# Down products of the last expert: rows 0 and 1 beside the up products, rows 2 and 3 behind them, one by one

## The chip, the cores and the metric

One core of one Trainium2 chip runs the whole program in one launch. The metric is the device time of one execution in microseconds (us); less is better. The core has five engines that run their own instruction streams and meet through semaphores: TensorE (PE in the profile, with its weight loads as PEld), VectorE (DVE), ScalarE (ACT), GpSimd (POOL) and SyncE (SP), the last of which starts most DMAs. An indirect DMA (one whose rows are addressed by a list of indices) is started by GpSimd.

## The reference

The input x is 4 sequences of 1024 tokens with 256 columns. Four steps follow, each on the layer norm of x and added to x: a mixing step, an expert step, causal attention, and the same expert step again.

```
def ffn(x, gate_w, w1, w2):            # n=4 sequences, t=1024, d=256, e=8 experts, k=256
    probs = softmax(einsum('ntd,ed->nte', x, gate_w))
    g, m = top_k(probs.transpose(0, 2, 1), k)      # each expert takes its best 256 tokens
    xin = x[batch_idx, m]                          # of each sequence
    h = gelu(einsum('nekd,edf->nekf', xin, w1))    # "up": 256 -> 1024
    h = einsum('nekf,efd->nekd', h, w2)            # "down": 1024 -> 256
    return zeros.at[batch_idx, m].add(g[..., None] * h)
x = x + mix(norm(x));  x = x + ffn(norm(x), ...)   # layer 0
x = x + attn(norm(x)); x = x + ffn(norm(x), ...)   # layer 1
```

The change lies in the last part of the second expert step.

## The kernel before

**Tiling of the expert step.** The four sequences are taken in two pairs. One pass n (0 to 15 in a layer) is one expert (n % 8) for one pair of sequences (n // 8): 512 gathered tokens, in four row groups j = 0 to 3 of 128 tokens each. Row groups 0 and 1 belong to the first sequence of the pair, 2 and 3 to the second. "The last expert" is the pass n = 15 of layer 1, the last work of the kernel.

**One pass.** The 1024 hidden columns are done in FT = 8 blocks f of 128.

- `up` (line 1311 holds its matmuls): for one f, 6 matmuls with 512 moving columns (2 halves of the 256 input columns, 3 products each, since each number is kept as a high and a low part) into PSUM bank 2 or 3 in turn, for all four row groups at once. ScalarE then takes the gelu out of the bank (line 1685), and VectorE writes the high part (2167) and the low part (2169) of h.
- `down` (line 1332): for one f, 4 row groups times 3 products = 12 matmuls with 256 moving columns. They add up over f = 0 to 7 in PSUM: row groups 0 and 1 in the two halves of bank 4, row groups 2 and 3 in those of bank 5. The first `down` of a pass waits (`take`) until both banks are drained; each `down` waits for the low part of h of its f.
- TensorE's order is written out in `experts`: `down` of f - 3 comes behind `up` of f (LAG = 3), so up 0, 1, 2, 3, down 0, up 4, down 1, up 5, down 2, up 6, down 3, up 7, down 4, 5, 6, 7. With the last `down`, bank 4 is signalled as filled behind the sixth of its 12 matmuls and bank 5 behind the twelfth.
- `scatter`: for each row group j, ScalarE multiplies the 128x256 result by the gate values into a tile f_yo (line 1694), and GpSimd starts an indirect DMA that adds its rows onto the output in HBM (line 2388). Row groups 0 and 1 wait for bank 4, row groups 2 and 3 for bank 5. GpSimd waits for ScalarE: for an even j through a count of its own (a_yo), for an odd j through the "drained" count of the bank. Before the first it also waits until the adds of the pass before have landed.

In every pass but the last the scatter stands beside the next pass's products. In the last one nothing comes behind it but the barrier: SyncE waits until all adds have landed (`stores_done`), each engine drains (line 428), and the program ends.

**Names.** `k.where[key]` says which bank a key such as ("down", layer, n, half) was given and as which use of it; `wait_filled` and `wait_drained` wait on that use. Bank 6 serves the routing of the pairs (route_ring) until that is over, and is not used in the last passes.

Of the kernel before, what the change touches and what calls it, by code (L numbers as in the profile page):

```python
# [15 lines left out]
P = 128  # L16
# [32 lines left out]
class Kernel:  # L49
# [282 lines left out]
    def tiles(self):  # L332
# [13 lines left out]
        self.t["early"].update({n: second[n] for n in ("tab", "idx", "row")})  # L346
        self.f = (first, second)

    def turned_block(self, t, i):

        flat = t["yT"][:].rearrange("p k l -> p (k l)")[:, i % 4 * BANK:(i % 4 + 1) * BANK]
        return flat.rearrange("p (s k l) -> p s k l", s=2, k=self.DT)
# [35 lines left out]
class Program:  # L388
# [26 lines left out]
    row_turn = row_scores = half_wide = count = digits = thresholds = threshold_rows = compare = rank = positions = skip  # L415
    hot_digits = hot_places = column = table = skip
    table_move = indices = skip
    weight_load = weight_high = weight_split = gather = xin = up = down = scatter = skip
    first_rows = rows_store = t_load = skip
    xt_block = qk_load = v_load = qk_product = qk_low = qk_double = v_product = skip  # L420
    row_max = part_max = max_rows = high_scores = scores = weigh = add_up = divide = sum_rows = scale_rows = skip
# [226 lines left out]
    def experts(self, layer, routed, gathered, turned):  # L648

        k, t = self.k, self.k.f[layer]  # L650
        LAG, N, FT = 3, 2 * k.E, k.FT
        if not gathered:
            self.gather(layer, 0, t)
        for _ in self.weights_ahead:
            pass
        if not turned:
            self.xin(layer, 0, t)
        yield
        for n in range(N):
            if n + 1 < N:  # L660
                routed(2 * layer + (n + 1) // k.E)
                self.gather(layer, n + 1, t)
            if n:
                for j in range(4):
                    self.scatter(layer, n - 1, j, t)
            for f in range(FT + LAG):
                if f < FT:
                    self.up(layer, n, f, t)
                    yield
                if f == FT - 1 and n + 1 < N:  # L670
                    self.xin(layer, n + 1, t)
                    self.turned = n + 1
                if f >= LAG:
                    self.down(layer, n, f - LAG, t)
                    yield
                part = f - LAG
                if 0 <= part < 4 and n + 1 < N:
                    self.weight_high(layer, n + 1, part, t)
                    self.weight_split(layer, n + 1, part, t)
                    if part % 2 and n + 2 < N:  # L680
                        self.weight_load(layer, n + 2, part // 2, t)
            self.through += 1
        for j in range(4):
            self.scatter(layer, N - 1, j, t)

    def stage_f(self, layer, before, behind):

        k, t = self.k, self.k.f[layer]
        self.norm_of, self.routed, self.loaded, self.through = {}, -1, 0, 0
        self.turned = 0  # L690
        first, second = iter(()) if layer else self.route(0), self.route(2 * layer + 1)
        self.weights_ahead = self.first_weights(layer)
        self.route_ring = [6, 7]
        gathered = turned = False
        self.route_uses = 1
        for n, _ in enumerate(before):
            pump(first)
            if layer and (n == 16 or 22 < n < 31 and n % 2 or n > 41):
                pump(self.weights_ahead)
            if self.routed == 2 * layer and not gathered and (layer == 0 or n > 41):  # L700
                self.gather(layer, 0, t)
                gathered = True
            if layer and n == 48:
                self.xin(layer, 0, t)
                turned = True
        for n, _ in enumerate(first):
            if n % 3 == 0 and self.loaded == 0:
                pump(self.weights_ahead)
        self.route_uses = 0

        def later():
            yield from second
            if layer == 0:
                while self.through < k.E:
                    yield
                self.first_rows()
                for _ in range(4):
                    yield
                self.norm_of["t", 0] = self.runs
                for _ in self.norm(k.t["xy"], k.t["xy"], t["stats"][0], t["mv"][0], t["rstd"][0], [(k.q_x, DMA)]):  # L720
                    for _ in range(4):
                        yield
            yield from behind
        later = later()

        def routed(r):
            while self.routed < r:
                next(later)
        for n, _ in enumerate(self.experts(layer, routed, gathered, turned)):
            pump(later)  # L730
        for _ in later:
            pass
# [296 lines left out]
class TensorE(Program):  # L1029
# [285 lines left out]
    def down(self, layer, n, f, t):  # L1315
# [20 lines left out]
        if f < FT - 1:  # L1336
            m.then_inc(k.pe_down, 1)

    def xt_block(self, b, c, dt):
# [192 lines left out]
class ScalarE(Reader):  # L1534
# [152 lines left out]
    def scatter(self, layer, n, j, t):  # L1687
        k, act = self.k, self.e
        b, h = 2 * (n // k.E) + j // 2, j % 2
        bank = self.wait_filled(("down", layer, n, j // 2))  # L1690
        if n:
            last = 2 * ((n - 1) // k.E) + j // 2
            self.wait_ge(k.q_add[last][h], DMA * (k.E * layer + (n - 1) % k.E + 1))
        act.mul(t["yo"][j][:], k.bank[bank][:, h * k.D:(h + 1) * k.D],
                t["tab"][b][:, n % k.E, h, 1:2]).then_inc(k.drained[bank] if h else k.a_yo, 1)
# [562 lines left out]
class GpSimd(Reader):  # L2258
# [114 lines left out]
    def scatter(self, layer, n, j, t):  # L2373
        k, pool = self.k, self.e
        b, h, e = 2 * (n // k.E) + j // 2, j % 2, n % k.E
        if h:
            self.wait_drained(("down", layer, n, j // 2))
        else:
            self.wait_ge(k.a_yo, 2 * (2 * k.E * layer + n) + j // 2 + 1)
        if e:  # L2380
            for i in range(2):
                self.wait_ge(k.q_add[b][i], DMA * (k.E * layer + e))
        elif layer:
            for c in range(k.NC):
                self.wait_ge(k.q_xout[c], DMA * (b + 1))
        else:
            self.wait_rows_stored(b // 2)
        pool.indirect_dma_start(
            out=(k.out if layer else k.res)[:, :],
            out_offset=bass.IndirectOffsetOnAxis(ap=t["row"][b][:, e, h:h + 1], axis=0),  # L2390
            in_=t["yo"][j][:], in_offset=None, compute_op=ALU.add).then_inc(k.q_add[b][h], DMA)
# [290 lines left out]
```

## Time and profile before

| what | us |
|---|---|
| median of the runs | 2219.75 (2218.33 to 2220.87, 3 runs) |
| the profiled execution: its own time | 2221.76 |
| its span in the trace | 2220.0 |
| PE busy in the span | 2142.3 (97%) |
| POOL busy in the span | 1374.8 (62%) |
| mean granted TensorE clock | 0.989 of full speed |

The profiled execution took 2221.76 us by the same clock as the runs; the trace covers 2220.0 of it, so 1.76 us lie around the span. Times below count from the span's start. Of a matmul the trace gives the start and a modelled end; successive matmuls overlap in it, so the distance between two starts is what one costs in a row of them.

### The profile page before, as it was taken

The page shows a single profiled execution, that of the slowest core. Times are in us where ns is not written, and L with a number is a line of the kernel's source. Part 1 is how long each engine was busy: PE and PEld are TensorE (multiplying, and loading weights), DVE is VectorE, ACT ScalarE, POOL GpSimd, SP SyncE. Part 2 cuts the span into 40 slices and gives each one's busy share as a digit, 9 for nine tenths or more (in the row PEclk, how much of TensorE's full clock was granted, in tenths as well). Part 3 has the DMA queues.
Part 4 walks back from the last instruction along what each step waited for, and adds up shares of the span by engine and source line. Part 5 has one row for each costly group of instructions (what it writes and reads, how often), then busy time and mean ns, then how long its engine had stood idle before and what let it go on. Part 6 is the DMA issues. An engine that isn't in the chain of part 4 may idle for free.

```text
span 2220.0 us, 34078 instructions
## 1 busy us (share of the span) xinstructions
PE 2142.3 (97%) x12130; PEld 1597.7 (72%) x12130; DVE 1463.3 (66%) x3344; ACT 1002.8 (45%) x1908; POOL 1374.8 (62%) x1242
## 2 busy tenths in 40 slices
PE   7998999999999999999999999999999999999997
PEld 5446888889876666766667666567666588899997
DVE  7375687776757666476775577874876646975553
ACT  6302543454355555255553355542555425444442
POOL 4313675777357676466664566663777846777774
PEclk9999999999999999999999999999999899999999
DMA  4524554555432221221222132222221245545552
GB/s 133 185 95 127 140 134 103 142 141 134 98 92 58 58 58 49 67 77 51 75 70 74 39 86 50 56 67 64 61 77 30 67 135 130 139 111 132 136 143 29
DMA packets 145048, 206.04 MB, mean 93 GB/s; under 512 B 19432, under 2 KB 112112, under 8 KB 144880
## 3 DMA queue, kind: packets, MB, share of 16 engines
q1 hardware_dynamic: 120304, 170.30, 25.7%
q0 software_dynamic: 24576, 33.57, 9.1%
q8 instruction: 97, 1.59, 0.3%
q14 instruction: 71, 0.58, 0.1%
HBM read 130.03 MB, written 39.85 MB: 77 GB/s over the span
## 4 chain that ended last, share of the span: by engine, by line
PE 74%; DVE 8%; POOL 4%; issue 3%; ACT 2%; DMA 1%; SPq 1%; POOLq 0%; DVEq 0%; ACTq 0%
PE psum L1311 12%; PE psum L1332 11%; PE psum L1458 11%; PE psum L1360 8%; PE psum L1423 7%; PE psum L1439 6%; PE psum L1483 5%; PE psum L1374 4%; PE psum L1388 3%; PE psum L1468 3%; POOL t_acc L2430 2%; DVE f_hlo L2169 1%; DVE f_hhi L2167 1%; PE psum L1401 1%; PE psum L1279 1%
## 5 line engine op out<-in xcount | busy, mean ns | idle before, releaser
L1734 ACT ACTIVATE t_p<-psum 128x512 f32<-128x512 f32 (+3 forms) x768 | 323.6, 492 | 294.1 <-PE psum L1439 285.8
L2430 POOL TENSOR_TENSOR t_acc<-t_acc,t_p 128x1024 f32<-128x1024 f32 (+3 forms) x256 | 417.0, 1629 | 14.5 <-ACT t_p L1734 0.5
L2349 POOL TENSOR_TENSOR f_wlo<-f_wst,f_whi 128x256 fp32r<-128x256 f32 x256 | 222.1, 944 | 149.8 <-ACT f_whi L1667 149.8
L1332 PE MATMUL psum<-f_whi,f_hhi 128*128 128x256 f32 x1024 | 295.4, 288 | 7.9 <-DVE f_hlo L2169 7.8
L1458 PE MATMUL psum<-t_p,t_v 128*64 128x512 f32 (+3 forms) x1536 | 289.1, 497 | 5.0 <-POOL t_p L2410 5.0
L1332 PE MATMUL psum<-f_whi,f_hlo 128*128 128x256 f32 x1024 | 289.9, 283 | 0.0
L1332 PE MATMUL psum<-f_wlo,f_hhi 128*128 128x256 f32 x1024 | 289.7, 283 | 0.0
L2167 DVE CAST f_hhi<-f_h 128x512 fp32r<-128x512 f32 x256 | 141.2, 552 | 207.0 <-ACT f_h L1685 206.2
L1685 ACT ACTIVATE f_h<-psum 128x512 f32<-128x512 f32 x256 | 153.0, 598 | 275.6 <-PE psum L1311 263.1
L1423 PE MATMUL psum<-t_qa,t_ka 128*128 128x512 f32 (+3 forms) x768 | 224.3, 372 | 1.8 <-DVE t_mx L2215 0.8
L2430 POOL TENSOR_TENSOR t_acc<-t_p 128x768 f32<-128x768 f32 x64 | 134.5, 2102 | 137.0 <-PE psum L1468 133.7
L1458 PEld LDWEIGHTS psum<-t_p,t_v 128*64 128x64 f32 x1536 | 99.2, 137 | 159.4 <-issue 141.3
L2410 POOL TENSOR_SCALAR_AFFINE_SELECT t_p<-t_p 128x256 f32<-128x256 f32 x256 | 105.0, 420 | 174.8 <-ACT t_p L1734 174.1
L1439 PE MATMUL psum<-t_qb,t_kb 65*128 65x512 f32 (+3 forms) x768 | 207.3, 352 | 4.8 <-DMA t_qb<-t_neg 4.4
L1311 PE MATMUL psum<-f_xhi,f_whi 128*128 128x512 f32 x512 | 204.8, 400 | 7.0 <-DVE f_xlo L2153 3.8
L1332 PEld LDWEIGHTS psum<-f_whi,f_hhi 128*128 128x128 f32 x1024 | 195.3, 191 | 16.7 <-DVE f_hlo L2169 9.6
L2169 DVE TENSOR_TENSOR f_hlo<-f_h,f_hhi 128x512 fp32r<-128x512 f32 x256 | 199.7, 780 | 8.8
L1311 PE MATMUL psum<-f_xlo,f_whi 128*128 128x512 f32 x512 | 202.1, 395 | 0.0
L1311 PE MATMUL psum<-f_xhi,f_wlo 128*128 128x512 f32 x512 | 201.0, 393 | 0.0
L1332 PEld LDWEIGHTS psum<-f_wlo,f_hhi 128*128 128x128 f32 x1024 | 195.4, 191 | 4.8
L1332 PEld LDWEIGHTS psum<-f_whi,f_hlo 128*128 128x128 f32 x1024 | 195.3, 191 | 0.0
L2221 DVE TENSOR_REDUCE t_mx<-psum 128x1 f32<-128x512 f32 x256 | 159.6, 683 | 41.5 <-PE psum L1388 38.9
(291 smaller groups left out, 4401.6 us busy)
## 6 DMA issues: line engine op xcount, KB each, us to landing
f_wst<-in_L_ffn_w SPq DMA_DIRECT2D x64, 1024.0 KB, 5.5
t_ka<-t_ka SPq DMA_DIRECT2D x64, 256.0 KB, 3.5
t_qb<-t_qa SPq DMA_DIRECT2D x64, 256.0 KB, 3.8
t_wk<-wkT SPq DMA_DIRECT2D x32, 256.0 KB, 4.1
t_wq<-wqT SPq DMA_DIRECT2D x32, 256.0 KB, 4.0
t_wv<-wvT SPq DMA_DIRECT2D x16, 512.0 KB, 4.7
normal<-f_xy SPq DMA_DIRECT2D x5, 1024.0 KB, 5.6
a_x<-in_L_attn_a_x SPq DMA_DIRECT2D x4, 1024.0 KB, 7.8
```

The source lines that it names most:

```text
L1311: m = pe.matmul(k.bank[b], w[:, dt, fs], x[:, dt, :], start=(dt == 0 and j == 0), stop=(dt == k.DT - 1 and j == 2))
L1332: m = pe.matmul(out, h[:, js], w[:, f, :], start=(f == 0 and a == 0 and j % 2 == 0), stop=(f == FT - 1 and a == 2), skip_group_check=True)
L1360: m = pe.matmul(k.bank[bank], w[:, part, ct, :], x[:, ct, cs], start=(ct == 0 and a == 0), stop=(ct == 1 and a == 2))
L1423: pe.matmul(k.bank[bank][:, q0:], hd["ka"][:, ks], hd["qa"][:, qs], start=True, stop=False)
L1439: pe.matmul(k.bank[banks[i]][:, q0:], hd["kb"][0:k.QROWS, ks], hd["qb"][0:k.QROWS, qs], start=False, stop=True).then_inc(k.filled[banks[i] ...
L1458: m = pe.matmul(k.bank[6][i * DH:(i + 1) * DH, q0:BANK], v[:, kt, vs:vs + DH], p[:, i, q0:BANK], start=(kt == 0), stop=(kt == last), skip_ ...
L1734: act.activation(p[:, i, q0:], k.bank[bank][:, q0:], ACT.Exp, scale=1.0 / float(np.sqrt(k.DH))).then_inc(k.drained[bank], 1)
L2167: dve.tensor_copy(hhi[:], h[:]).then_inc(k.d_h.sem, 1)
L2169: dve.tensor_tensor(hlo[:], h[:], hhi[:].bitcast(F32), ALU.subtract).then_inc(k.d_h.sem, 1)
L2221: s = dve.tensor_reduce(mx1[:, i, n - k.KPC:n - k.KPC + 1], part, AX.X, ALU.max)
L2349: m = pool.tensor_tensor(t["wlo"][n % 2][:, i, ks], t["wst"][:, i, ks], t["whi"][n % 2][:, i, ks].bitcast(F32), ALU.subtract)
L2430: pool.tensor_tensor(acc[:, :, q0:], (p0 if kt == 1 else acc)[:, :, q0:], p[:, :, q0:], ALU.add).then_inc(k.p_acc, 1)
```

## The change

The passes before the last one stay as they are. In the last one (layer 1, n = 15), `experts` calls `last_expert`:

- beside the up products, with the same lag of 3, only row groups 0 and 1 of the down products are done (6 matmuls per f in place of 12);
- behind up 7 come: row groups 0 and 1 for f = 4 (within the loop), 5 and 6; row group 2 for f = 0 to 3; row groups 0 and 1 for f = 7; row group 2 for f = 4 to 7; row group 3 for f = 0 to 7;
- row group 2 stays in bank 5, row group 3 goes into bank 6, each signalled as filled when its own f = 7 is done. ScalarE and GpSimd wait for row group 3 by the key of bank 6;
- the number of matmuls and their shapes stay the same. The count pe_down is not raised in this pass; only a next pass would wait for it.

```diff
+    def down_key(self, layer, n, j):
+        return "down", layer, n, 2 if layer and n == 2 * self.E - 1 and j == 3 else j // 2
...
                 for j in range(4):
                     self.scatter(layer, n - 1, j, t)
+            if layer and n == N - 1:
+                yield from self.last_expert(layer, n, t)
+                continue
...
+    def last_expert(self, layer, n, t):
+        LAG, FT = 3, self.k.FT
+        for f in range(FT):
+            self.up(layer, n, f, t)
+            yield
+            if f >= LAG:
+                self.down_rows(layer, n, f - LAG, (0, 1), t)
+                yield
+        for f in range(FT - LAG, FT - 1):
+            self.down_rows(layer, n, f, (0, 1), t)
+        for f in range(4):
+            self.down_rows(layer, n, f, (2,), t)
+        self.down_rows(layer, n, FT - 1, (0, 1), t)
+        for f in range(4, FT):
+            self.down_rows(layer, n, f, (2,), t)
+        for f in range(FT):
+            self.down_rows(layer, n, f, (3,), t)
...
+    def down_rows(self, layer, n, f, js, t):          # TensorE
...
+        key = k.down_key(layer, n, js[0])
+        if f == 0:
+            self.take(key, 4 + key[3])
...
+        self.wait_ge(k.d_h.sem, k.d_h.at(FT * N + f, "lo"))
+        for j in js:
+            out, rows = k.bank[bank][:, (j % 2) * D:(j % 2 + 1) * D], slice(j * P, (j + 1) * P)
+            for a, (h, w) in enumerate(((t["hhi"][f], w2h), (t["hhi"][f], w2l), (t["hlo"][f], w2h))):
+                m = pe.matmul(out, h[:, rows], w[:, f, :], start=(f == 0 and a == 0 and j == js[0]),
+                              stop=(f == FT - 1 and a == 2), skip_group_check=True)
+        if f == FT - 1:
+            m.then_inc(k.filled[bank], 1)
...
     def scatter(self, layer, n, j, t):                # ScalarE
-        bank = self.wait_filled(("down", layer, n, j // 2))
+        bank = self.wait_filled(k.down_key(layer, n, j))
...
     def scatter(self, layer, n, j, t):                # GpSimd
         if h:
-            self.wait_drained(("down", layer, n, j // 2))
+            self.wait_drained(k.down_key(layer, n, j))
```

## Rows read from the trace of the kernel before

**Rows 1.** The page: busy time of the engines, and busy tenths in 40 slices

```profile
PE 2142.3 (97%) x12130; PEld 1597.7 (72%) x12130; DVE 1463.3 (66%) x3344; ACT 1002.8 (45%) x1908; POOL 1374.8 (62%) x1242
...
PE   7998999999999999999999999999999999999997
```

**Rows 2.** The chain of work that ended last, from 2180 us: start, us, what

```profile
2200.17 1.39 PE psum L1311 x6
2201.55 5.05 PE psum L1332 x42
2206.60 0.02 issue
2206.62 0.48 ACT f_yo L1694
...
2212.93 1.55 POOL out L2388
```

**Rows 3.** Timeline of GpSimd, the last two passes' scatters: start, us, what, idle before

```profile
2190.47 1.76 POOL L2388 DMA_INDIRECT out<-f_yo,f_row  x1 [0.30 <-DMA out<-f_yo,f_row]
2207.37 1.55 POOL L2388 DMA_INDIRECT out<-f_yo,f_row  x1 [15.14 <-ACT f_yo L1694]
2209.22 1.55 POOL L2388 DMA_INDIRECT out<-f_yo,f_row  x1 [0.30 <-issue]
2211.08 1.55 POOL L2388 DMA_INDIRECT out<-f_yo,f_row  x1 [0.30 <-issue]
2212.93 1.55 POOL L2388 DMA_INDIRECT out<-f_yo,f_row  x1 [0.30 <-issue]
```

**Rows 4.** Drains at the end (line 428), then the first instruction behind the barrier: count, ns

```profile
L428 PEldq DRAIN  x1: 2345/2345/2345, 2205.0 to 2205.0; - x1
...
L428 POOLq DRAIN  x1: 10987/10987/10987, 2208.5 to 2208.5; - x1
L428 SPq DRAIN  x1: 7/7/7, 2216.7 to 2216.7; - x1
...
L2654 SPq COMPARE_BRANCH  x1: 38/38/38, 2219.5 to 2219.5; - x1
```

**Rows 5.** Timeline of TensorE, the last pass: up 7, then down 7's first, sixth, last

```profile
2200.00 0.40 PE L1311 MATMUL psum<-f_xhi,f_whi 128*128 128x512 f32 x1
...
2201.16 0.39 PE L1311 MATMUL psum<-f_xhi,f_wlo 128*128 128x512 f32 x1
2201.39 0.28 PE L1332 MATMUL psum<-f_whi,f_hhi 128*128 128x256 f32 x1
...
2205.70 0.28 PE L1332 MATMUL psum<-f_whi,f_hhi 128*128 128x256 f32 x1
2205.82 0.28 PE L1332 MATMUL psum<-f_wlo,f_hhi 128*128 128x256 f32 x1
2205.94 0.28 PE L1332 MATMUL psum<-f_whi,f_hlo 128*128 128x256 f32 x1
2206.06 0.28 PE L1332 MATMUL psum<-f_whi,f_hhi 128*128 128x256 f32 x1
...
2206.30 0.28 PE L1332 MATMUL psum<-f_whi,f_hlo 128*128 128x256 f32 x1
...
2207.02 0.28 PE L1332 MATMUL psum<-f_whi,f_hlo 128*128 128x256 f32 x1
```

**Rows 6.** Busy time by stretch (PE, PEld, DVE, ACT, POOL), granted clock, DMA share, GB/s

```profile
2201.40:2207.30 5.90, 5.90 (x49) 5.70 (x47) 1.12 (x2) 1.27 (x3) 0.00 (x0) 1.00 0.00 0
...
2216.00:2217.00 1.00, 0.00 (x0) 0.00 (x0) 0.00 (x0) 0.00 (x0) 0.00 (x0) 0.50 0.10 13
2217.00:2218.00 1.00, 0.00 (x0) 0.00 (x0) 0.00 (x0) 0.00 (x0) 0.00 (x0) 0.50 0.00 0
```

**Rows 7.** Timelines of ScalarE and VectorE, the last pass: gelu and h of f = 7, the scatter

```profile
2201.59 0.60 ACT L1685 ACTIVATE f_h<-psum 128x512 f32<-128x512 f32 x1 [2.22 <-PE psum L1311]
2206.62 1.57 ACT L1694 ACTIVATE f_yo<-psum,f_tab 128x256 f32<-128x256 f32 x4 [4.44 <-PE psum L1332]
...
2202.29 0.43 DVE L2167 CAST f_hhi<-f_h 128x512 fp32r<-128x512 f32 x1 [1.67 <-ACT f_h L1685]
2202.75 0.69 DVE L2169 TENSOR_TENSOR f_hlo<-f_h,f_hhi 128x512 fp32r<-128x512 f32 x1
```

**Rows 8.** DMAs issued from 2203 to 2212 us, then from 2212.9: count, us to landing

```profile
out<-f_yo,f_row POOLq DMA_INDIRECT x3, 3.7
...
out<-f_yo,f_row POOLq DMA_INDIRECT x1, 3.7
```

**Rows 9.** Instructions on f_yo from 2100 us: ns min/median/max, then landing

```profile
L2388 POOL DMA_INDIRECT out<-f_yo,f_row x21: 1548/1760/1795, 2098.3 to 2212.9; - x21
L1694 ACT ACTIVATE f_yo<-psum,f_tab x20: 466/474/479, 2114.0 to 2207.7; 128x256 f32<-128x256 f32 x20
...
DMA to landing us min/median/max: 3.7/4.0/5.2
```

More of the change, by code:

```diff
@@ L417 @@
     table_move = indices = skip
-    weight_load = weight_high = weight_split = gather = xin = up = down = scatter = skip
+    weight_load = weight_high = weight_split = gather = xin = up = down = down_rows = scatter = skip
     first_rows = rows_store = t_load = skip
@@ L1337, in down @@
             m.then_inc(k.pe_down, 1)
+    def down_rows(self, layer, n, f, js, t):
+        k, pe = self.k, self.e
+        D, FT = k.D, k.FT
+        N = 2 * k.E * layer + n
+        key = k.down_key(layer, n, js[0])
+        if f == 0:
+            self.take(key, 4 + key[3])
+            self.wait_ge(k.d_split, 2 * N + 2)
+            self.wait_ge(k.p_split, 2 * N + 2)
+        bank, _ = k.where[key]
+        w2h = t["whi"][n % 2][:, 1].rearrange("p (k d) -> p k d", k=FT)
+        w2l = t["wlo"][n % 2][:, 1].rearrange("p (k d) -> p k d", k=FT)
+        self.wait_ge(k.d_h.sem, k.d_h.at(FT * N + f, "lo"))
[6 more added lines that the diff above has]
+            m.then_inc(k.filled[bank], 1)
     def xt_block(self, b, c, dt):
```

## The prediction

> **What bounds the kernel now.** The page comes first: TensorE is busy for 97% of the span [rows 1], so nearly everywhere the time is its stream of matmuls, and of that stream the change removes nothing. The last of the 40 slices of PE is not full, though: at 55.5 us a slice, the tenth that is missing has to be looked for at the end. So the chain of waits comes second, read from its end backwards [rows 2]: TensorE until 2206.60, one product of ScalarE (the gate of row group 0), then GpSimd to 2212.93 + 1.55 = 2214.48. The third view is GpSimd's timeline [rows 3]. The reader is to see that its four indirect DMAs stand back to back: 1.55 us each and 0.30 of issue between them, starts 2207.37, 2209.22, 2211.08, 2212.93, a pitch of 5.56 / 3 = 1.853 us. Only the first waits for ScalarE; the other three wait for GpSimd itself. Last come the drains [rows 4]: SP leaves its wait for the adds at 2216.7, GpSimd's drain ends at 2208.5 + 11.0 = 2219.5, and all engines go on at 2219.5.
>
> So the last 13.4 us (2220.0 less 2206.6) are a serial tail: first gate product, four DMA issues in a row, a last piece of 2220.0 - 2214.48 = 5.52 us for landing, drain and end. Its start is set by the moment at which bank 4 (row groups 0 and 1) is full. TensorE itself is full until its last matmul ends at 2207.02 + 0.28 = 2207.30 [rows 5], with no idle time and at a granted clock of 1.00, the 2.4 GHz level [rows 6].
>
> **The change part by part.**
>
> *TensorE's stream.* Before and after there are 48 up and 96 down matmuls in the pass. From 2205.70 to 2207.02 there are 11 distances, 0.120 us for one down matmul; the up ones go (2201.16 - 2200.00) / 5 = 0.232 apart [rows 5]. The sum is the same, so TensorE ends at 2207.30 again if nothing makes it wait. Two things could: banks and h.
>
> *h of f = 7.* Its low part is ready at 2202.75 + 0.69 = 2203.44 [rows 7], which is 2.05 after the end of up 7's issue (2201.39 [rows 5]). After the change up 7 comes earlier by the 4 x 6 = 24 down matmuls that are left out ahead of it (f = 0 to 3), 24 x 0.120 = 2.88: issued by 2198.51, h ready at 2200.56. Between it and the down product that needs it stand 6 x 3 (f = 4, 5, 6 of row groups 0 and 1) + 12 (row group 2, f = 0 to 3) = 30 matmuls, 3.60 us: 2202.11. That leaves 1.55 us, so no wait. For the earlier f the distance is larger (three ups and three short downs, 3 x (1.39 + 0.72) = 6.3 us, against the same 2.05). If that cover were gone, each microsecond of lateness would cost one.
>
> *The up products come closer together*, 1.39 + 0.72 = 2.11 us apart instead of 2.82. Their banks alternate, so one is needed again one up and two short downs after it was filled, 2.8 us, and the gelu that frees it starts 0.20 after the up's issue ended and takes 0.60 [rows 5, 7]. VectorE has 0.43 + 0.69 = 1.12 us of work per f [rows 7]. Both fit.
>
> *Banks.* Bank 5 is now asked for later than before, and ScalarE and GpSimd had emptied it before the issue at 2190.47 [rows 3]; bank 6 was last used by the routing, which was over passes ago. No wait on either, I take 0. A gain is excluded, since TensorE had no idle time to lose; a loss could only be a late bank 6, and it would be the same at the end up to the 1.24 us found below.
>
> *When bank 4 is full.* Behind its last matmul there are now 12 (row group 2, f = 4 to 7) + 24 (row group 3) = 36 matmuls instead of 6. It is full 30 x 0.120 = 3.60 us earlier. By the same distances its last matmul starts at 2207.02 - 36 x 0.120 = 2202.70, ScalarE starts at about 2203.02 (before, 2206.30 to 2206.62 [rows 5, 7]) and GpSimd's first DMA 0.75 later [rows 3, 7], at 2203.77. VectorE did its last work at 2200.56, so it stands beside nothing there. The adds of the pass before, for which GpSimd waits, had their last issue at 2190.47 [rows 3]; with the longest landing of 5.2 [rows 9] that is 2195.7, long done.
>
> *The other three.* Row group 1: ready with the first. Row group 2: its bank is full 24 matmuls before the end, at 2207.30 - 2.88 = 2204.42; with 0.04 to ScalarE and 0.75 more, GpSimd could start at 2205.2, and its turn is at 2203.77 + 2 x 1.853 = 2207.48. Row group 3: full at 2207.30, could start at 2208.09; its turn is at 2203.77 + 3 x 1.853 = 2209.33. So GpSimd's own pace still decides, by 1.24 us, and the last DMA starts at 2209.33 instead of 2212.93: 3.60 us earlier. Moving the first one by more would have bought at most the 4.84 us between 2212.93 and 2208.09; past that TensorE's end decides.
>
> *The price of a DMA issue.* The rows give 1548 to 1795 ns [rows 9]. The short ones are those at the end, with VectorE idle; the one at 2190.47 in between took 1.76 [rows 3]. After the change the first two run beside TensorE's matmuls. I take 1.55, as at 2207.37, because VectorE is idle there too; if TensorE's stream made them long (1.79), four times 0.24 = 0.96 would be lost and 2.6 gained. The lower bound is the pitch as it is; nothing in the rows is shorter than 1548.
>
> *Landing and drain.* The last DMA took 3.7 us to land [rows 8], in a stretch where the queue had only its neighbours, at the same pitch as after. The longest on this path was 5.2 [rows 9], when weights and gathers ran too; none do here. SP's release at 2216.7 is 2.2 after the last issue ended, GpSimd's drain ends 5.0 after it [rows 4]. I take both as tied to the last DMA, so they move by the whole 3.60.
>
> Sum: -3.60 us. The profiled execution's span becomes 2216.4 and its own time 2218.2; the median of the runs shown lies 2.0 below the profiled time and becomes 2219.75 - 3.60 = 2216.15, take 2216.2 (-0.16%).
>
> **The rivals.**
>
> *A: the end is not tied to the last DMA.* GpSimd's drain starts at 2208.5, before three of the four DMAs have been issued, and is shown as 11.0 us long [rows 4]. It starts 0.3 after ScalarE's last gate product (2206.62 + 1.57 = 2208.19 [rows 7]). If that length were the drain's own, the end would hang on the last gate product, which TensorE's unchanged end sets. That product would now be alone: 2207.34 to 2207.81, drain from 2208.1 to 2219.1, gain 0.4 us, time 2219.4. For it: the data have landed at 2216.7 and traffic ends in the slice before 2217 [rows 6], yet the drain goes on for 2.8 us. Against it: it has to outlast work that stands ahead of it in GpSimd's queue. The Trainium skill ("PSUM — Partial Sum Buffer", Engine vs sequencer instructions) says that a drain waits until its engine is fully idle; by that rule the drain is a wait behind the last DMA and the forecast holds, by a fixed length from its own start it would be 2219.4. The trace cannot tell them apart, since there is one such drain.
>
> *B: single row groups run slower (the other side).* Row groups 2 and 3 now put 24 matmuls in a row into one 128x256 region, where before it was 3. If each had to wait for the one before to end, they would go 0.28 apart instead of 0.12 [rows 5], 48 x 0.16 = 7.7 us more: TensorE ends at 2215.0, the last DMA starts at 2215.8, 2.8 later than before, time 2222.6. It decides from a distance at which the 48 cost over 4.84 us, that is 0.22 us apart. Against it: within a group of three the starts are 0.12 apart, just as between groups [rows 5], and up puts six in a row into one region at 0.232, well under their 0.39. Nothing speaks for it.
>
> *C: the first DMAs run long beside TensorE* and the landing takes the median 4.0 in place of 3.7: gain 3.6 - 0.96 - 0.3 = 2.3 us, time 2217.4.
>
> *D: the order is right but some wait on h or a bank delays bank 4* by more than the 1.55 us of slack, say 2 us late: 0.5 us lost, 3.1 gained, time 2216.6. It is inside the forecast's own range.
>
> **How the numbers follow.** The forecast with D has 0.75, C 0.11, A 0.10, B 0.04. The forecast's own range is 2214.9 to 2217.4, the gain of 3.6 with the 1.3 us by which the runs shown lie about their median. A measurement of this kernel tells a change from none at about 0.2%, here 4.4 us. The forecast is 3.6, so it lies within that bound but near it; with the spread of the runs a little over a third of the forecast's share would read as more than 4.4: faster 0.28, slower 0.03 (most of B is itself only 2.8 us), same 0.69. Range with the rivals: 2214.3 to 2218.9, which leaves out A's end and B.
>
> **What would show it.** In the profile after: TensorE without idle time until about 2207.3; ScalarE's first gate product near 2203.0 and its last alone near 2207.3; four DMAs at a pitch of 1.85 from 2203.8, the last at 2209.3 with 0.3 of issue ahead of it and not a wait for ScalarE; SP's release near 2213.1 and GpSimd's drain ending near 2215.9 while it still starts near 2208. A drain that ends near 2219 would be A; down matmuls more than 0.12 apart would be B; issues of 1.75 us C. A wait on VectorE ahead of down 7 would break the step on h.

## The result and the profile after

The changed kernel takes 2216.53 us (median of 18 runs, 2214.75 to 2221.86) against 2220.53 (18 runs, 2218.07 to 2224.3): ratio 0.9984, 95% interval 0.9977 to 0.9990. The ratio stands for 3.6 us; the two medians lie 4.0 us apart. The forecast was 2216.2. Its profiled execution took 2218.82 us, with a span of 2217.0.

GpSimd's timeline after, first the last add of the pass before, then the four of the last pass (start, us, what, idle before). It answers to [rows 3]:

```profile
2191.07 1.76 POOL L2436 DMA_INDIRECT out<-f_yo,f_row  x1 [0.30 <-issue]
2204.37 1.55 POOL L2436 DMA_INDIRECT out<-f_yo,f_row  x1 [11.54 <-ACT f_yo L1742]
2206.22 1.55 POOL L2436 DMA_INDIRECT out<-f_yo,f_row  x1 [0.30 <-issue]
2208.08 1.55 POOL L2436 DMA_INDIRECT out<-f_yo,f_row  x1 [0.30 <-issue]
2209.93 1.55 POOL L2436 DMA_INDIRECT out<-f_yo,f_row  x1 [0.30 <-issue]
```

The same four, at the same pitch, 3.00 us earlier. ScalarE's side of it, answering to [rows 7]:

```profile
2199.31 0.60 ACT L1733 ACTIVATE f_h<-psum 128x512 f32<-128x512 f32 x1 [1.50 <-PE psum L1337]
2203.62 0.84 ACT L1742 ACTIVATE f_yo<-psum,f_tab 128x256 f32<-128x256 f32 x2 [3.72 <-PE psum L1382]
2205.07 0.47 ACT L1742 ACTIVATE f_yo<-psum,f_tab 128x256 f32<-128x256 f32 x1 [0.60 <-PE psum L1382]
2207.94 0.47 ACT L1742 ACTIVATE f_yo<-psum,f_tab 128x256 f32<-128x256 f32 x1 [2.40 <-PE psum L1382]
```

The four gate products have come apart: two when bank 4 is full, one for bank 5, one for bank 6 behind TensorE's end. TensorE's first and last down matmuls in the tail of the pass, and the busy time by stretch (PE, PEld, DVE, ACT, POOL, clock, DMA share, GB/s), answering to [rows 5, 6]:

```profile
2199.11 0.28 PE L1382 MATMUL psum<-f_whi,f_hhi 128*128 128x256 f32 x1
...
2207.62 0.28 PE L1382 MATMUL psum<-f_whi,f_hlo 128*128 128x256 f32 x1
```

```profile
2200.00:2207.90 7.90, 7.90 (x66) 7.70 (x65) 1.12 (x2) 1.31 (x3) 3.10 (x2) 1.00 0.14 17
2207.90:2217.00 9.10, 0.00 (x1) 0.00 (x0) 0.00 (x0) 0.47 (x1) 3.10 (x2) 0.66 0.40 43
```

From 2199.11 to 2207.62 there are 71 distances of 0.120 us; TensorE has no idle time, at a granted clock of 1.00. VectorE made the low part of h for f = 7 here, and the four adds took this long to land:

```profile
2200.47 0.69 DVE L2217 TENSOR_TENSOR f_hlo<-f_h,f_hhi 128x512 fp32r<-128x512 f32 x1
```

```profile
DMA to landing us min/median/max: 3.7/3.8/3.9
```

The drains, answering to [rows 4]:

```profile
L432 POOLq DRAIN  x1: 8031/8031/8031, 2208.5 to 2208.5; - x1
L432 SPq DRAIN  x1: 7/7/7, 2213.8 to 2213.8; - x1
...
L2702 SPq COMPARE_BRANCH  x1: 38/38/38, 2216.5 to 2216.5; - x1
```

GpSimd's drain starts at 2208.5 in both traces, but is 3 us shorter. It starts 0.3 us behind the end of ScalarE's last product again; that product now stands alone, so this is 0.6 us behind TensorE's end where it was 1.2.

TensorE's end T (end of the last matmul) is the fixed point from which such a tail has to be read. It lies at 2207.30 before and at 2207.62 + 0.28 = 2207.90 after, since this execution had come to the last pass 0.60 us later: the eight transposes of the pass start at 2178.18 before (first line) and at 2178.78 here (second):

```profile
2178.18 0.87 PE psum L1292 x8
```

```profile
2178.78 0.87 PE psum L1318 x8
```

The pass itself takes 29.12 us in both. The tail, span less T, is 2220.0 - 2207.30 = 12.70 before and 2217.0 - 2207.90 = 9.10 after: 3.60 us shorter, of which 3.00 show in the span. In the traces of the experiments T lies between 2202.9 and 2213.9, which is more than any edit is worth, while the tail of a kernel traced twice came out alike within 0.1 us (9.10 and 9.11, 7.56 and 7.58). So the tails carry the verdicts, one trace each, and the ratios of the runs only have to agree.

### The profile page after: what moved, and what is told of

It reads as the page before. It is cut to its first block, busy times and chain, and to the rows that moved or that the text cites. A ratio compares the mean times of both kernels' runs of the same rounds, so it can differ in the third digit from the quotient of the medians.

```text
span 2217.0 us, 34079 instructions
## 1 busy us (share of the span) xinstructions
PE 2144.5 (97%) x12130; PEld 1600.3 (72%) x12130; DVE 1463.6 (66%) x3344; ACT 1003.0 (45%) x1908; POOL 1375.0 (62%) x1242
## 4 chain that ended last, share of the span: by engine, by line
PE 74%; DVE 8%; POOL 4%; issue 3%; ACT 2%; DMA 1%; SPq 1%; POOLq 0%; DVEq 0%; ACTq 0%
PE psum L1337 12%; PE psum L1506 11%; PE psum L1358 11%; PE psum L1408 8%; PE psum L1471 7%; PE psum L1487 6%; PE psum L1531 5%; PE psum L1422 4%; PE psum L1436 3%; PE psum L1516 3%; POOL t_acc L2478 2%; DVE f_hhi L2215 2%; DVE f_hlo L2217 1%; PE psum L1449 1%; DVE f_wlo L2190 1%
## 5 line engine op out<-in xcount | busy, mean ns | idle before, releaser
L1358 PE MATMUL psum<-f_whi,f_hhi 128*128 128x256 f32 x992 | 286.4, 289 | 7.1 <-DVE f_hlo L2217 7.0
L1358 PE MATMUL psum<-f_whi,f_hlo 128*128 128x256 f32 x992 | 280.8, 283 | 0.0
L1358 PE MATMUL psum<-f_wlo,f_hhi 128*128 128x256 f32 x992 | 280.6, 283 | 0.0
L1358 PEld LDWEIGHTS psum<-f_whi,f_hhi 128*128 128x128 f32 x992 | 189.1, 191 | 15.6 <-DVE f_hlo L2217 9.0
L1358 PEld LDWEIGHTS psum<-f_wlo,f_hhi 128*128 128x128 f32 x992 | 189.3, 191 | 4.6
L1358 PEld LDWEIGHTS psum<-f_whi,f_hlo 128*128 128x128 f32 x992 | 189.2, 191 | 0.0
```

The costliest lines, as they stand in the source:

```text
L1358: m = pe.matmul(out, h[:, js], w[:, f, :], start=(f == 0 and a == 0 and j % 2 == 0), stop=(f == FT - 1 and a == 2), skip_group_check=True)
```

## The experiments

All but the last start from the changed kernel. What came out, in us; "last add" is the start of the last indirect DMA against T:

| kernel | T | last add | tail | ratio to the kernel before, 95% interval |
|---|---|---|---|---|
| before | 2207.30 | T + 5.63 | 12.70 | 1 |
| changed | 2207.90 | T + 2.03 | 9.10 | 0.9984 (0.9977 to 0.9990) |
| e1 shared bank | 2204.08 | T + 2.64 | 9.72 | 0.9986 (0.9977 to 0.9995) |
| e2 later | 2202.85 | T + 4.19 | 11.25 | 0.9988 (0.9979 to 0.9997) |
| e3 first | 2209.73 | T + 0.79 | 7.87 | 0.9983 (0.9974 to 0.9992) |
| e4 no add of group 1 | 2208.81 | T + 0.78 | 7.79 | 0.9983 (0.9974 to 0.9992) |
| e5 = e3 + e4 | 2211.10 | T + 0.79 | 7.80 | 0.9977 (0.9968 to 0.9986) |
| e6 no adds of groups 2, 3 | 2213.42 | T - 1.68 | 5.98 | 0.9970 (0.9957 to 0.9982) |
| e7 = e3, no last barrier | 2210.14 | T + 0.78 | 7.56 | 0.9979 (0.9969 to 0.9988) |
| e8 changed, again | 2213.89 | T + 2.03 | 9.11 | 0.9982 (0.9973 to 0.9991) |
| e9 no adds in the pass | 2207.18 | none | 5.82 | one run each |
| e10 = e7 + early drain | 2213.89 | T + 0.79 | 5.01 | 0.9968 (0.9956 to 0.9980) |
| e11 = e7, again | 2213.82 | T + 0.78 | 7.58 | 0.9979 (0.9970 to 0.9988) |
| e12 before + early drain | 2205.52 | T + 5.62 | 10.28 | 0.9983 (0.9974 to 0.9992) |

Every interval leaves 1 out, so each version that has one is faster than the kernel before. Every interval also overlaps the changed kernel's, so the runs alone do not tell the versions apart. The times expected of e1 to e4 were 2217.1, 2218.7, 2215.3 and 2215.3; the medians were 2216.74, 2218.16, 2216.50 and 2215.86, so e3 missed its time by 1.2 us though its tail came as expected. In the code cuts below `...` marks what is left out.

**e1_shared_bank: row group 3 back in bank 5.**

```diff
-        return "down", layer, n, 2 if layer and n == 2 * self.E - 1 and j == 3 else j // 2
+        return "down", layer, n, j // 2
...
-        if f == 0:
+        if f == 0 and js[0] != 3:
             self.take(key, 4 + key[3])
...
-        if f == FT - 1:
+        if f == FT - 1 and js[0] != 2:
             m.then_inc(k.filled[bank], 1)
```

The start flag of row group 3 is dropped too. Bank 5 is so taken once, by row group 2, and signalled as filled once, behind the last matmul of row group 3.

> The order of the changed kernel, but row group 3 shares bank 5 with row group 2, signalled once behind the last matmul. Measured from the end of TensorE's last matmul (T), the changed kernel starts its last add at T + 2.03 us and the span ends at T + 9.10. Theory (the end is the later of GpSimd's turn and readiness): ScalarE's products 2 and 3 start at T + 0.04 and T + 0.40, the third add at T + 0.79, the last at T + 2.64; tail 9.7, time 0.6 above the changed kernel's (about 2217.1). Rival (the own bank buys nothing, since GpSimd's pace sets the end): tail 9.1, time unchanged.

GpSimd's third add now waits for ScalarE, and the chain is broken in its middle:

```profile
2202.40 1.55 POOL L2436 DMA_INDIRECT out<-f_yo,f_row  x1 [0.30 <-issue]
2204.86 1.55 POOL L2436 DMA_INDIRECT out<-f_yo,f_row  x1 [0.92 <-ACT f_yo L1742]
2206.72 1.55 POOL L2436 DMA_INDIRECT out<-f_yo,f_row  x1 [0.30 <-issue]
```

The wait is 0.92, of it 0.30 would have been issue anyway: the own bank is worth 0.62 us of the 3.60 (9.72 against 9.10), and the order without it brings the other 2.98.

**e2_later: row groups 0 and 1 finished 18 matmuls later.**

```diff
-        for f in range(4):
+        for f in range(FT):
             self.down_rows(layer, n, f, (2,), t)
+        for f in range(2):
+            self.down_rows(layer, n, f, (3,), t)
         self.down_rows(layer, n, FT - 1, (0, 1), t)
-        for f in range(4, FT):
-            self.down_rows(layer, n, f, (2,), t)
-        for f in range(FT):
+        for f in range(2, FT):
             self.down_rows(layer, n, f, (3,), t)
```

> Row groups 0 and 1 of f = 7 come behind all of row group 2 and two f of row group 3, so that 18 matmuls follow them in place of 36. Theory (GpSimd's chain starts when bank 4 is full, 0.12 us per matmul moved): first add 18 x 0.12 = 2.16 us later against T, last add at T + 4.19, tail 11.3, time about 2218.7 (1.4 us gained on the kernel before). Rival (the gain comes from the banks of their own and the single row groups, not from where row groups 0 and 1 end): tail 9.1, time 2216.5.

```profile
2202.57 0.28 PE L1382 MATMUL psum<-f_whi,f_hlo 128*128 128x256 f32 x1
```

```profile
2207.04 1.55 POOL L2436 DMA_INDIRECT out<-f_yo,f_row  x1 [0.30 <-issue]
```

Tail 11.25 against 9.10: 2.15 us for 18 matmuls, 0.119 each. Banks and single row groups are as in the changed kernel; what is lost hangs on the moment at which bank 4 is full.

**e3_first: row groups 0 and 1 finished at once.**

```diff
-        for f in range(FT - LAG, FT - 1):
+        for f in range(FT - LAG, FT):
             self.down_rows(layer, n, f, (0, 1), t)
-        for f in range(4):
-            self.down_rows(layer, n, f, (2,), t)
-        self.down_rows(layer, n, FT - 1, (0, 1), t)
-        for f in range(4, FT):
+        for f in range(FT):
             self.down_rows(layer, n, f, (2,), t)
         for f in range(FT):
```

> Behind up 7 row groups 0 and 1 are finished at once (f = 4 to 7), then row group 2, then 3: 48 matmuls follow bank 4. Theory: GpSimd's turn for the last add would be T + 0.59, row group 3 is ready at T + 0.79, so the end is now set by TensorE's end: tail 9.10 - 1.24 = 7.9, time about 2215.3. The low part of h for f = 7 is ready 2.05 us behind up 7 and is wanted after 18 matmuls, 2.16 us: no stall. Rival (h is late, TensorE stalls ahead of down 7): TensorE has idle time there and ends later by it, and the gain of 1.2 shrinks by as much; above 1.2 us of stall it is slower than the changed kernel.

```profile
2208.47 1.55 POOL L2433 DMA_INDIRECT out<-f_yo,f_row  x1 [0.30 <-issue]
2210.52 1.55 POOL L2433 DMA_INDIRECT out<-f_yo,f_row  x1 [0.50 <-ACT f_yo L1739]
```

The last add now waits for ScalarE, 0.20 us beyond the usual 0.30: GpSimd's pace has given the end back to TensorE, as worked out. The tail is 1.23 us shorter. The cover over h has shrunk to nothing, which shows in TensorE's timeline as one distance of 0.18 in place of 0.12:

```profile
2202.92 0.28 PE L1379 MATMUL psum<-f_whi,f_hlo 128*128 128x256 f32 x1
2203.04 0.34 PE L1379 MATMUL psum<-f_whi,f_hhi 128*128 128x256 f32 x1
2203.22 0.28 PE L1379 MATMUL psum<-f_wlo,f_hhi 128*128 128x256 f32 x1
```

The pass takes 29.18 instead of 29.12 (2180.55 to 2209.73). The low part of h was ready at 2202.25 + 0.69 = 2202.94:

```profile
2202.25 0.69 DVE L2214 TENSOR_TENSOR f_hlo<-f_h,f_hhi 128x512 fp32r<-128x512 f32 x1
```

Only 0.11 of slack had been counted. So the four f of row group 2 that the changed kernel puts ahead of down 7 save it 0.06 us of TensorE, and cost it 1.23 us of tail.

**e4_no_add_1 and e5_first_no_add_1: one add fewer**, in the order of the changed kernel and in that of e3. The diff is that of e6 below, with (1,).

> The changed kernel without the last pass's add of row group 1 (its gate product and its wait stay; the output lacks that add). Theory (GpSimd's pace of 1.853 us per add sets the last start, up to the 1.24 us at which row group 3's readiness takes over): last add at T + 0.79, tail 7.9, time about 2215.3. Rival (an add costs its full pitch at the end): last add at T + 0.18, which is impossible before its product is there; (the adds are hidden): tail 9.1.

> Row groups 0 and 1 finished at once (as in e3_first) and the last pass's add of row group 1 left out. Theory (both changes shorten the same thing, GpSimd's turn, and past 1.24 us TensorE's end decides): nothing on top of either alone, last add at T + 0.79, tail 7.8 to 7.9. Rival (the two gains are independent): tail 9.10 - 1.24 - 1.3 = 6.6.

The last add in e4:

```profile
2209.59 1.55 POOL L2438 DMA_INDIRECT out<-f_yo,f_row  x1 [0.85 <-ACT f_yo L1742]
```

Tails 7.79 and 7.80. Taking away 1.85 us of GpSimd's work is worth 1.31 on the changed order and nothing on e3's; both run into the same floor, T + 0.79.

**e6_no_add_23: what the drain waits for.**

```diff
+        if layer and n == 2 * k.E - 1 and j in (2, 3):
+            return
         pool.indirect_dma_start(
...
-                    self.wait_ge(k.q_add[b][h], DMA * k.E * 2)
+                    gone = 2 * (b - 2) + h in (2, 3)
+                    self.wait_ge(k.q_add[b][h], DMA * (k.E * 2 - gone))
```

The return stands behind GpSimd's waits and ahead of the add; the other lines make SyncE wait for as many adds as there are. The output lacks the adds left out, here and in e4, e5 and e9.

> The changed kernel without the last pass's adds of row groups 2 and 3; their gate products stay, and GpSimd still waits for them, so that its drain starts where it did, 0.6 us behind TensorE's end (T). Theory (the drain is a wait for the last add: 5.0 us behind the end of its issue, here at T - 0.13): drain ends at T + 4.9, tail 5.4. Rival (the drain takes a length of its own from its start): it ends at T + 8.6 as in the changed kernel, tail 9.1.

Neither number came. The tail was 5.98:

```profile
L432 POOLq DRAIN  x1: 4834/4834/4834, 2214.0 to 2214.0; - x1
L432 SPq DRAIN  x1: 7/7/7, 2215.7 to 2215.7; - x1
```

The rival of a length from its own start (9.1) is out. But the drain ends 5.5 us behind the last issue (2213.29), not 5.0, and 4.8 behind its own start.

**e9_no_add: no add in the last pass at all.** The same edit with (0, 1, 2, 3).

> The changed kernel without any add in the last pass; the gate products and GpSimd's waits for them stay. The last software DMA has then landed some 10 us before GpSimd's drain starts, 0.6 us behind TensorE's end. In the run without the last two adds the drain ended 5.5 us behind the last issue and 4.8 behind its own start, against 5.0 behind the last issue in all others. Theory 1 (once GpSimd's queue is empty the drain takes 4.8 to 5.0 us of its own, landing or not): drain 4.8 us long, tail 5.9. Theory 2 (the drain waits some 3 us behind the last landing): it is under 1 us long, tail about 2.

```profile
2190.34 1.76 POOL L2438 DMA_INDIRECT out<-f_yo,f_row  x1 [0.30 <-issue]
...
L432 SPq DRAIN  x1: 7/7/7, 2194.4 to 2194.4; - x1
...
L432 POOLq DRAIN  x1: 4671/4671/4671, 2207.8 to 2207.8; - x1
```

SyncE sees all adds landed at 2194.4, 13 us before GpSimd's drain starts, and the drain still takes 4.67 us. So in this trace the drain is no wait for landing: it takes 4.7 us of its own, from when GpSimd has nothing else left. The same 4.7 us behind the 0.30 that follow an issue would give the 5.0 behind the last issue in the traces with all four adds.

**e7_first_no_barrier** (and e11, the same kernel again): is it the explicit drain?

```diff
-        self.barrier()
+        self.stores_done(2)
```

> e3_first without the last barrier of the kernel's own: SyncE still waits for all adds, but no engine drains of its own ahead of the program's end. Theory (the 2.8 us between the last landing and the end of GpSimd's drain belong to GpSimd's queued adds, whichever drain asks for them; the program's end drains too): tail 7.9 less at most the 0.5 us of the second round, 7.4 to 7.9. Rival (the explicit drain itself costs them): tail 7.9 - 2.8 = 5.1.

> e7_first_no_barrier once more on the same chip as e10: tail 7.56, time 1.5 us below the changed kernel's, so about 0.9978 of the kernel before.

Tails 7.56 and 7.58. The drain at the program's end takes over the full length:

```profile
L2699 POOLq DRAIN  x1: 6787/6787/6787, 2210.7 to 2210.7; - x1
```

That is as long as in e3. Only 0.3 us, the way through the barrier itself, is gone (7.87 to 7.56).

**e8_changed_again**

> The changed kernel once more, on the chip of the three above. Tail 9.1 again; time 1.3 us above e5_first_no_add_1. TensorE's end itself, which lay at 2207.3 before and 2207.9 after in the traces, may lie elsewhere by some microseconds, since it lay between 2202.9 and 2209.7 in the traces of the four kernels run so far, and not by what they change.

Tail 9.11, 0.01 from the first trace, with T 6.0 us later. Against e5 the median of the runs was 2.9 us higher (2223.63 and 2220.75), not 1.3; the ratios, 0.9982 and 0.9977, lie 1.1 us apart with overlapping intervals, and the traces show 1.31.

**e10_early_drain: the drain taken out beside TensorE.**

```diff
+        if layer and n == 2 * k.E - 1 and j == 0:
+            pool.drain()
```

It stands in GpSimd's `scatter`, ahead of the waits and adds of the last pass.

> e7_first_no_barrier with one more drain of GpSimd ahead of the last pass's adds, where GpSimd is idle for some 10 us. The drain at the end took 4.7 us even where no software DMA was open. Theory 1 (every drain of GpSimd behind software DMAs costs 4.7 us): the last one again ends 5.0 us behind the last issue, tail 7.6 as in e7. Theory 2 (the 4.7 us clear up what has gathered since the drain before, over the whole kernel): the early one takes them, the last one is short, and the end is set by the last landing, tail about 5.1 to 5.6.

First the early drain; then the last add of the pass before and the last add of all; then the program's last drain and SyncE's first instruction behind its wait for the adds:

```profile
L2422 POOLq DRAIN  x1: 10907/10907/10907, 2192.5 to 2192.5; - x1
```

```profile
2197.01 1.76 POOL L2435 DMA_INDIRECT out<-f_yo,f_row  x1 [0.30 <-issue]
...
2214.68 1.55 POOL L2435 DMA_INDIRECT out<-f_yo,f_row  x1 [0.50 <-ACT f_yo L1739]
```

```profile
L2701 POOLq DRAIN  x1: 4162/4162/4162, 2214.4 to 2214.4; - x1
L2701 SPq COMPARE_BRANCH  x1: 38/38/38, 2218.5 to 2218.5; - x1
```

The early drain ends at 2203.4, 4.6 us behind the issue that ended at 2198.77: nearly the whole price, paid where GpSimd idles until 2208.93. The last one ends at 2218.56, 2.3 behind the last issue instead of 5.0, together with the landing for which SyncE waits. Tail 5.01, 7.7 us shorter than before and 4.1 shorter than in the changed kernel, with three edits of which the early drain is worth 2.57 (7.58 in e11 to 5.01; the medians of these two lie 2.6 us apart). By its runs this version beats the kernel before, ratio 0.9968 (0.9956 to 0.9980). That it also beats the changed kernel rests on the tail: the two intervals still touch.

**e12_before_early_drain: the early drain alone, on the kernel before.**

> The kernel before with nothing but the early drain of GpSimd, ahead of the last pass's adds. Theory (the last drain's own 4.7 us come out beside TensorE, and with them the 2.8 us between SyncE's release and the end of GpSimd's drain; independent of the order of the down products): last add at T + 5.6 as before, tail 12.7 - 2.6 = 10.1. Rival (the early drain only paid in e10 because the program's last barrier was gone as well): tail 12.7.

```profile
2211.14 1.55 POOL L2390 DMA_INDIRECT out<-f_yo,f_row  x1 [0.30 <-issue]
...
L428 POOLq DRAIN  x1: 8492/8492/8492, 2206.7 to 2206.7; - x1
```

```profile
L2377 POOLq DRAIN  x1: 10909/10909/10909, 2184.2 to 2184.2; - x1
```

The early drain (second view) ends at 2195.1, long before the first add of the last pass.

Tail 10.28, 2.42 us shorter than before, last add at T + 5.62 unchanged; the drain ends 2.5 behind the last issue. By the tails, two lines that leave the order alone bring two thirds of what the change does.

## Why the prediction was right

- **The bound.** Right: a serial tail of 13.4 us whose start is the moment at which bank 4 is full. e2 and e3 move that moment both ways and the tail follows at 0.12 us per matmul, until the floor. The whole gain of e3, 12.70 - 7.87 = 4.83 us, is the 4.84 that was given as the most to be had.
- **TensorE's stream.** Right: the same number of matmuls, 0.120 apart, no stall, the pass 29.12 us long in both traces. h of f = 7 was ready at 2200.47 + 0.69 = 2201.16 and wanted 3.6 us behind 2199.11, at 2202.7: 1.55 of slack as counted. e3 took 1.44 of it away and came out at the edge.
- **The first add.** Forecast 3.60 us earlier against TensorE: it stood at T + 0.07 before and stands at T - 3.53.
- **GpSimd's pace as the bound, with 1.24 us to spare.** Right, shown from both sides: e4 takes work off GpSimd and gains 1.31, e3 starts it earlier and gains 1.23, and e5 with both gains 1.30. The own bank for row group 3 is a sixth of the gain (e1).
- **The price of an issue.** The number was right, 1.55 us beside TensorE too, but the reason given, that VectorE is idle there, is not borne out. In the pass before, an add took 1.55 us with VectorE at work for 1.12 of them, and the next took 1.57 (trace of the kernel before):

```profile
2186.74 1.55 POOL L2388 DMA_INDIRECT out<-f_yo,f_row  x1 [0.30 <-issue]
2188.59 1.57 POOL L2388 DMA_INDIRECT out<-f_yo,f_row  x1 [0.30 <-issue]
```

```profile
2186.93 0.43 DVE L2167 CAST f_hhi<-f_h 128x512 fp32r<-128x512 f32 x1 [5.08 <-ACT f_h L1685]
2187.39 0.69 DVE L2169 TENSOR_TENSOR f_hlo<-f_h,f_hhi 128x512 fp32r<-128x512 f32 x1
```

  What makes others 1.76 to 1.79 long stays open.
- **Landing and drain tied to the last add.** The sum was right, since against T the release moved by 3.5 us and the drain's end by 3.6, and the alternative of a drain with a length from its own start (forecast 2219.4 us) fell with the first trace of the changed kernel. The reason given was only half of it. The Trainium skill ("PSUM — Partial Sum Buffer", Engine vs sequencer instructions) says that a drain waits until its engine is fully idle. The traces agree that it waits: in the changed kernel it starts at 2208.5, ahead of the last issue at 2209.93, and ends at 2216.5. But e9 shows 4.67 us of a drain with GpSimd idle, and e10 that behind an earlier drain the last one ends 2.7 us sooner (2.3 behind the last issue, not 5.0). The forecast needed only that it follows the last issue; a forecast for an edit that empties GpSimd early would have been wrong by it, as e6's was, by 0.6 us.
- **Rivals B, C and D.** B (single row groups slower) is out: 0.120 apart through 24 in a row. C is out: 1.55 us for every issue beside TensorE and landings of 3.7 to 3.9. D did not occur.
- **The number.** 2216.2 forecast, 2216.53 measured. The gain of 3.60 came out in the tail, but that the medians agree to 0.3 us is in part luck: the runs of the changed kernel spread over 7 us, and the forecast started from a median of 3 runs, 2219.75, that 18 runs put at 2220.53. The change of 0.16% lies within the 0.2% bound that had most of the chance; with 18 runs on each side its sign is clear of noise.

**Left open:** what the 4.7 us of GpSimd's drain at the end do. The drain at the first barrier, ahead of all its indirect DMAs, took 0.89 us (the 887 ns here, the first of two drains in the trace after):

```profile
L432 POOLq DRAIN  x2: 887/4459/8031, 3.3 to 2208.5; - x2
```

One that followed four adds behind an early drain ended 2.3 us behind the last issue. Whether the length grows with the number of DMAs since the last drain, or is paid once, no run here tells. Nor is it shown that the DMAs are the reason: the first barrier also stands ahead of GpSimd's other work on the data, and no run took that work away. The changed order with nothing but the early drain was not run either.

## What to carry to other kernels

At the end of a kernel, look not for the busiest engine but for the serial chain behind its end, and ask of each link whether it could have started earlier: order the last products so that what a slow issuer must send one by one becomes ready one by one, and stop when its last turn meets the readiness of the last piece (here 1.24 us beyond what the change took). Measure such a tail from a fixed point in the trace, since the time ahead of it varies by more than the edit is worth. And look at the drains: one placed where GpSimd idles anyway took 2.4 to 2.6 us off the end.

## What was not expected of the hardware

GpSimd's drain at the end of this kernel takes 4.7 us of its own even when all its indirect DMAs have landed 13 us before (4.67 us in e9), and an earlier drain in idle time takes most of what that cost adds to the end (tail 7.58 to 5.01 in e10, 12.70 to 10.28 in e12).
